# Low parts of the expert weights: GpSimd alone, and the last three experts' behind the block table

## The chip, the core and the metric

The kernel runs on one core of a Trainium2 chip. The metric is the device time of one execution in microseconds. Five engines take part: TensorE (PE), VectorE (DVE), ScalarE (ACT), GpSimd (POOL) and SyncE (SP, which here only issues DMAs). Each runs its own queue in order and waits on semaphores.

## The reference

Sixteen images of 96 x 96 are cut into 36 patches each, embedded (width 192) and joined by a class token: 16 x 37 = 592 tokens. One attention block follows (12 heads, causal mask, rotary positions), then a mixture of experts:

```
gates = softmax(x @ Wg + bg);  topk_g, topk_i = top_k(gates, 2)      # 8 experts
h = gelu(x @ W1[e] + b1[e])            # 192 -> 768
y = h @ W2[e] + b2[e]                  # 768 -> 192
out = x + sum over the two chosen experts of gate * y
```

## The kernel before

**Tokens.** The 592 tokens are worked on in TILES = 6 tiles of up to 111 tokens. Embedding, projections and rotary come first, then a software pipeline over the tiles i = 0 to 6, in which each engine's order is written out by hand: scores, softmax, values and output projection of tile i or i - 1, and the second norm and the gating of tile i - 3. The last tiles' gating follows it as a straight chain: `second_stats`, `norm_apply`, `gates_t`, `logits`, `choose`, `ranks`, `rows`.

**Dispatch.** For each tile DVE (`rows`, L1159) finds the row of each chosen (token, expert) pair, and GpSimd scatters the normed tokens to DRAM with two indirect DMAs (`dispatch`, L398, L405), which count up `scattered`. After the last tile DVE computes the block table (L1222 to L1242): how many blocks of 128 rows each expert has, and for each of up to NB = 17 blocks its expert (`T_EXP`) and first row (`T_ROW`). `table_ready` releases the rest. With the inputs used 14 blocks are live.

**Weights.** An expert's weights are 32-bit numbers and are used as a high and a low part: ACT rounds the raw weights to `F32R` (`round_w1`, `round_w2`; semaphores `w1_hi`, `w2_hi`), and the low part is the raw number less the high one. GpSimd makes the low parts of `w2` of all experts (`split_w2`, L380, 1152 columns) and those of `w1` of experts 0 to 4 (`split_w1`, L386 and L388, 768 columns each); both count up `lo_pool`. DVE makes those of `w1` of experts 5, 6 and 7 (its own `split_w1`, L1024 and L1026, `lo_dve`), after the table and ahead of the first block. EARLY = 6 experts are loaded and rounded during the attention; the raw weights of experts 6 and 7 lie where the attention's buffers were and are loaded by SP once `early_free` is set.

**GpSimd's order** (L408 to L449): in loop step i `root` and `dispatch` of tile i - 3 and i - 4 and the splits of expert i - 1; then `root(4)`, the bias rows of experts 6 and 7 (L395, L396, two DMAs that it issues), `split_w2(5)`, `root(5)`, `dispatch(3)` to `dispatch(5)`, `split_w2(6)`, `split_w2(7)`, and then for each block the indirect DMA that adds the block's output into `out` (L446). `root` computes 1/sqrt of the variance, for which DVE waits in `norm_apply` (L1012 to L1015).

**SP after the table:** the stores of `h` (L353), the waits for `scattered` (L356), the loads of the table's values (L305, L360), and then the load of each block's rows into `xin` (L364).

**The blocks.** For block b: TensorE transposes `xin` (`block_t`, L695, L696); ACT rounds it (L935 to L937); DVE makes the low part (`tokens_low`, L1253, L1254, which read PSUM, and set `xlo_ready`); TensorE computes `layer1` (ten matmuls of 384 columns, L708), ACT the gelu (L947), TensorE transposes (`hidden_t`, L718) and computes `layer2` (L732, L734), ACT and DVE make the output (L964, L1281). In DVE's queue `block_gates(b)` stands ahead of `tokens_low(b)`: a copy of the token numbers (L1261), and two small operations whose inputs are all in SBUF (L1262, L1265), for the gates. TensorE loads the block's expert into a register (`expert_of`, L738) a block ahead. While it waits for the table it runs nothing; then come 18 warm-up matmuls (L743), `block_t(0)`, and waits for all low parts of all experts, `lo_dve` for 3 and `lo_pool` for 13.

Of the kernel before, what the change touches and what calls it, by code (L numbers as in the profile page):

```python
# [23 lines left out]
ALU = mybir.AluOpType  # L24
# [11 lines left out]
DA, DB = 128, D - 128  # L36
# [4 lines left out]
E = 8  # L41
F = 768
# [8 lines left out]
NB = (2 * N - E) // BLK + E  # L51
# [4 lines left out]
A_HI, A_LO, B_HI, B_LO, W2_HL = 0, F, 2 * F, 3 * F, 4 * F  # L56
WCOLS = 4 * F + FC * 2 * D
EARLY = 6
# [5 lines left out]
FH = F // 2  # L64
LAG = 3

T_EXP, T_ROW, T_LIVE, T_COLS = 0, NB, 2 * NB, 2 * NB + 1


class Region:  # L70
# [15 lines left out]
def vit_block(nc, patches, w_tok, tok_rows, tok_sel, w_qkv_a, w_qkv_b, rope_cos, rope_sin, mask,  # L86
# [4 lines left out]
    with ctx:  # L91
        def sem(name):
            return ctx.enter_context(nc.semaphore(name))
# [61 lines left out]
        table = keep("table", [128, NB])  # L155
        tablei = keep("tablei", [128, T_COLS], I32)
# [3 lines left out]
        we = Region(nc, w_at, top)("we", [128, E, WCOLS], F32R)  # L160

        raw = [Region(nc, w_at + e * WCOLS * 4, top)(f"raw{e}", [128, WCOLS], F32) for e in range(E)]
# [11 lines left out]
        tmp_nb = scratch("tmp_nb", [128, 2, NB])  # L174
# [96 lines left out]
        table_ready = sem("table_ready")  # L271
        padded = sem("padded")
        w1_hi = sem("w1_hi")
# [2 lines left out]
        b1_raw = sem("b1_raw")  # L276
        b1_lo = sem("b1_lo")
        b1_rows = sem("b1_rows")
        lo_dve = sem("lo_dve")
        lo_pool = sem("lo_pool")  # L280
        early_free = sem("early_free")
        xin_ld = [sem(f"xin_ld{b}") for b in range(2)]
# [19 lines left out]
        def blocks_in_use(engine):  # L302

            engine.wait_ge(table_ready, 1)
            live = engine.value_load(tablei[0:1, T_LIVE:T_LIVE + 1], min_val=MINB, max_val=NB)  # L305
            return lambda b: engine.If(live > b) if b >= MINB else nullcontext()
# [59 lines left out]
        @block.gpsimd  # L366
        def _(pool):
            def root(t, rnd):

                n = ROWS[t]  # L370
                pool.wait_ge(veps_ready, rnd * TILES + t + 1)
                nc.gpsimd.tensor_tensor(rstd[0:n, t:t + 1], veps[0:n, t:t + 1], nhalf[0:n, :], ALU.pow)\  # L372
                    .then_inc(rstd_ready, 1)

            def split_w2(e):

                pool.wait_ge(w2_hi, e + 1)
                hl = we[:, e, W2_HL:WCOLS].rearrange("p (f c) -> p f c", c=2 * D)
                whole = raw[e][:, W2_HL:WCOLS].rearrange("p (f c) -> p f c", c=2 * D)
                nc.gpsimd.tensor_tensor(hl[:, :, D:2 * D], whole[:, :, D:2 * D], hl[:, :, 0:D], ALU.subtract)\  # L380
                    .then_inc(lo_pool, 1)

            def split_w1(e):

                pool.wait_ge(w1_hi, e + 1)
                nc.gpsimd.tensor_tensor(we[:, e, A_LO:A_LO + F], raw[e][:, A_LO:A_LO + F], we[:, e, A_HI:A_HI + F],  # L386
                                        ALU.subtract)
                nc.gpsimd.tensor_tensor(we[0:DB, e, B_LO:B_LO + F], raw[e][0:DB, B_LO:B_LO + F],  # L388
                                        we[0:DB, e, B_HI:B_HI + F], ALU.subtract).then_inc(lo_pool, 1)

            def bias_rows(e0, e1):
                if e1 > EARLY:
                    pool.wait_ge(early_free, 1)

                pool.dma_start(we[DB:DB + 1, e0:e1, B_LO:B_LO + F], b1[e0:e1, :]).then_inc(b1_rows, 16)  # L395
                pool.dma_start(we[DB + 1:DB + 2, e0:e1, B_LO:B_LO + F], b1lo_sb[e0:e1, :]).then_inc(b1_rows, 16)  # L396

            def dispatch(t):  # L398

                n = ROWS[t]  # L400
                pool.wait_ge(row_ready, t + 1)
                if t == 0:
                    pool.wait_ge(padded, 16)
                for j in range(2):
                    pool.indirect_dma_start(xs, bass.IndirectOffsetOnAxis(ap=rowu[0:n, t, j:j + 1], axis=0),  # L405
                                            pay[0:n, t % 3, :], None).then_inc(scattered[t % 3], 16)

            pool.wait_ge(fixed, 1)  # L408
            nc.gpsimd.memset(vp[:, :, :, HD:HD + 1], 1.0).then_inc(ones_ready, 1)
            for t in range(TILES):  # L410
                root(t, 0)
            for t in range(TILES):
                n = ROWS[t]
                pool.wait_ge(rope_ready, t + 1)
                nc.gpsimd.tensor_tensor(qk[0:n, t, :], ropec[0:n, t % 2, :], ropes[0:n, t % 2, :], ALU.add)\
                    .then_inc(qk_ready, 1)
                pool.wait_ge(v2_ready, t + 1)
                nc.gpsimd.tensor_tensor(vp[0:n, t, :, PC:VC],
                                        vr[0:n, t % 2, :].rearrange("p (h d) -> p h d", d=HD),
                                        vp[0:n, t, :, HD + 1:PC], ALU.subtract).then_inc(v3_ready, 1)  # L420
            pool.wait_ge(b1_lo, 1)
            bias_rows(0, EARLY)
            for i in range(TILES + 1):
                if i >= LAG:
                    root(i - LAG, 1)
                if i >= LAG + 1:
                    dispatch(i - LAG - 1)
                if 1 <= i < EARLY:
                    split_w1(i - 1)
                    split_w2(i - 1)  # L430
            root(TILES - 2, 1)
            bias_rows(EARLY, E)
            split_w2(EARLY - 1)
            root(TILES - 1, 1)
            dispatch(TILES - 3)
            dispatch(TILES - 2)
            dispatch(TILES - 1)
            for e in range(EARLY, E):
                split_w2(e)
            pool.wait_ge(out_first, 16 * (TILES + 1))  # L440
            used = blocks_in_use(pool)
            for b in range(NB):
                with used(b):
                    pool.wait_ge(y_ready, b + 1)
                    pool.wait_ge(gate_ready, b + 1)
                    pool.indirect_dma_start(out, bass.IndirectOffsetOnAxis(ap=tokblk[:, b:b + 1], axis=0),  # L446
                                            y[:, b % 2, :], None, compute_op=ALU.add).then_inc(added, 16)

                    pool.wait_ge(added, 16 * (b + 1))  # L449

        @block.tensor
        def _(pe):
# [245 lines left out]
            def layer1(b, expert):  # L698

                pe.wait_ge(xlo_ready, b + 1)  # L700
                for hf in range(2):
                    if b >= 1:
                        pe.wait_ge(gelu_done, 2 * b - 1 + hf)
                    parts = ((xahi, A_HI), (xalo, A_HI), (xahi, A_LO), (xb1, B_HI), (xb2, B_LO))
                    for i, (x, c) in enumerate(parts):
                        rows = x.shape[0]
                        w = we[0:rows, bass.ds(expert, 1), c + hf * FH:c + hf * FH + FH].rearrange("p e c -> p (e c)")
                        last = mm(bank[1 + hf][:, 0:FH], x[:, :], w, start=(i == 0), stop=(i == 4))  # L708
                    last.then_inc(l1_done, 1)
# [33 lines left out]
                mm(bank[3][:, 0:FH], we[:, 0, A_HI:A_HI + 128], we[:, 0, A_HI:A_HI + FH], start=True, stop=True)  # L743
            pe.wait_ge(early_free, 1)
            block_t(0)
            pe.wait_ge(lo_dve, E - EARLY + 1)
            pe.wait_ge(lo_pool, E + EARLY - 1)
            pe.wait_ge(b1_rows, 64)
            expert = expert_of(0)
            layer1(0, expert)  # L750
# [234 lines left out]
        def _(dve):  # L985
            v = nc.vector
            steps = [0]

            def step(ins):
                steps[0] += 1  # L990
                ins.then_inc(dve_step, 1)
                dve.wait_ge(dve_step, steps[0])
# [25 lines left out]
            v.memset(nhalf[:, :], -0.5).then_inc(fixed, 1)  # L1018
            v.memset(hn2tb[DB:DB + 1, :, :], 1.0).then_inc(fixed, 1)

            def split_w1(e):

                dve.wait_ge(w1_hi, e + 1)
                v.tensor_tensor(we[:, e, A_LO:A_LO + F], raw[e][:, A_LO:A_LO + F], we[:, e, A_HI:A_HI + F],  # L1024
                                ALU.subtract)
                v.tensor_tensor(we[0:DB, e, B_LO:B_LO + F], raw[e][0:DB, B_LO:B_LO + F],  # L1026
                                we[0:DB, e, B_HI:B_HI + F], ALU.subtract).then_inc(lo_dve, 1)

            for t in range(TILES + 1):
                if t < TILES:  # L1030
                    dve.wait_ge(h_copied, t + 1)
# [148 lines left out]
            for i in range(TILES + 1):  # L1180
# [29 lines left out]
                if i >= LAG:  # L1210
# [24 lines left out]
            step(v.tensor_reduce(tmp_nb[:, :, :], passed[:, :, :, :], AX.X, ALU.add))  # L1235
            step(v.scalar_tensor_tensor(out=tmp_nb[:, 1, :], in0=blockids_sb[:, :], scalar=float(BLK),
                                        in1=tmp_nb[:, 1, :], op0=ALU.mult, op1=ALU.add))
            v.tensor_scalar(table[:, :], tmp_nb[:, 0, :], float(E - 1), None, ALU.min)
            v.tensor_copy(tablei[:, T_LIVE:T_LIVE + 1], ends[:, E - 1:E])
            v.tensor_scalar(tablei[:, T_EXP:T_EXP + NB], tmp_nb[:, 0, :], float(E - 1), None, ALU.min)  # L1240
            v.tensor_scalar(tablei[:, T_ROW:T_ROW + NB], tmp_nb[:, 1, :], float(SPARE), None, ALU.min)\
                .then_inc(table_ready, 1)  # L1242

            for t in range(TILES - 3, TILES):
                add_bias2(t)

            for e in range(EARLY - 1, E):
                split_w1(e)

            def tokens_low(b):  # L1250

# [130 lines left out]
```

## Time and profile before

| | before |
|---|---|
| time, median of 3 runs | 245.99 us (243.65 to 252.13) |
| the profiled execution | 244.32 us |
| its span | 242.5 us |
| PE / PEld / DVE / ACT / POOL busy | 75% / 58% / 63% / 43% / 40% |
| granted TensorE clock, mean | 0.802 |

The profile's span runs from the first to the last instruction; PEld is TensorE's weight load, which overlaps PE. [...] In the rows below `a<-b` is output and inputs of an instruction by the program's names, `x` a count, and the bracket at the end is the engine's idle time before it and what ended that. All times start at the span's start.

### The profile page before, as it was taken

The numbers are of one execution on the slowest core, as the hardware profiler recorded it, in microseconds if no ns is written. First come the engines' busy times: TensorE is split into PE (matmuls) and PEld (weight loads), VectorE is DVE, ScalarE is ACT, GpSimd is POOL, SyncE is SP. The second block draws the span as 40 slices with busy tenths as digits, with TensorE's granted clock in tenths as the row PEclk, the third lists the DMA queues.
The fourth block names the chain that finished last, engine by engine and source line by source line (L and its number), as shares of the span: only waits on it lengthen the run. The fifth ranks groups of instructions, "written<-read, shape, count | busy, mean of one in ns | idle before, by whom it ended". The sixth has DMA issues, their size and how long they took to land.

```text
span 242.5 us, 3838 instructions
## 1 busy us (share of the span) xinstructions
PE 182.8 (75%) x1065; PEld 140.7 (58%) x1065; DVE 153.4 (63%) x436; ACT 104.4 (43%) x313; POOL 96.1 (40%) x77
## 2 busy tenths in 40 slices
PE   3999999659799499729829343454899999999830
PEld 2887343245666295615815122254799999999720
DVE  0133756859878968797994888996356455564410
ACT  2011333477687366527030022900656566566500
POOL 1012265739404600853925736930023233433241
PEclk9999999977587956955555555559999999999995
DMA  6945999999999400100100795202032342422211
GB/s 164 312 111 138 278 285 279 285 279 251 201 194 210 112 3 1 39 0 4 39 0 13 213 278 143 50 26 76 22 63 38 59 59 42 67 52 20 33 19 16
DMA packets 25656, 27.12 MB, mean 112 GB/s; under 512 B 4880, under 2 KB 21928, under 8 KB 25634
## 3 DMA queue, kind: packets, MB, share of 16 engines
q1 hardware_dynamic: 21378, 24.16, 40.1%
q0 software_dynamic: 4256, 2.69, 7.8%
q8 instruction: 11, 0.18, 0.3%
q14 instruction: 11, 0.09, 0.1%
HBM read 23.73 MB, written 8.64 MB: 133 GB/s over the span
## 4 chain that ended last, share of the span: by engine, by line
PE 50%; DVE 23%; DMA 10%; issue 8%; ACT 3%; SPq 2%; POOL 1%; ACTq 0%; POOLq 0%; DVEq 0%
PE bank L708 8%; DMA out_y<-y,tokblk 7%; PE bank L463 6%; PE bank L534 5%; PE bank L732 4%; PE bank L489 4%; DVE sneg L1091 3%; DVE ao L1118 3%; PE bank L718 3%; DVE tablei L1240 3%; PE bank L495 2%; PE bank L734 2%; PE bank L550 2%; DVE pay L1015 2%; DMA wtok_sb<-in_w_tok 1%
## 5 line engine op out<-in xcount | busy, mean ns | idle before, releaser
L446 POOL DMA_INDIRECT out_y<-y,tokblk x14 | 21.9, 1562 | 55.2 <-DVE y L1281 23.8
L372 POOL TENSOR_TENSOR rstd<-veps,nhalf 111x1 f32<-111x1 f32 (+1 forms) x12 | 7.0, 584 | 58.5 <-DVE veps L999 58.5
L732 PE MATMUL bank<-we,hthi 128*128 x84 | 25.9, 371 | 1.4 <-DVE htlo L1272 1.4
L827 ACT ACTIVATE probs<-bank,sneg 111x111 f32<-111x111 f32 (+1 forms) x72 | 18.2, 347 | 18.2 <-DVE sneg L1091 18.1
L380 POOL TENSOR_TENSOR we<-raw,we 128x1152 fp32r<-128x1152 f32 x8 | 20.9, 2617 | 4.8 <-ACT we L883 4.7
L1091 DVE TENSOR_SCALAR sneg<-smax 111x4 f32<-111x4 f32 (+1 forms) x18 | 21.0, 1166 | 0.6
L708 PE MATMUL bank<-we,xahi 128*128 x56 | 20.2, 361 | 1.4 <-DVE xb L1254 1.4
L405 POOL DMA_INDIRECT dispatched<-pay,rowu x12 | 16.5, 1373 | 11.9 <-DVE rowu L1167 10.1
L734 PE MATMUL bank<-we,htlo 128*128 x84 | 21.1, 251 | 0.0
L463 PE MATMUL bank<-wtok_sb,x_sb 128*111 128x192 f32 (+1 forms) x72 | 17.5, 403 | 4.1 <-DMA wtok_sb<-in_w_tok 4.1
L947 ACT ACTIVATE hid<-bank 128x384 f32<-128x384 f32 x28 | 13.8, 492 | 10.2 <-PE bank L708 10.2
L463 PEld LDWEIGHTS bank<-wtok_sb,x_sb 128*111 128x111 f32 (+1 forms) x72 | 13.9, 208 | 6.7 <-DMA wtok_sb<-in_w_tok 4.7
L550 PE MATMUL bank<-ident_sb,probs 111*111 111x111 f32 (+1 forms) x72 | 13.5, 346 | 5.2 <-ACT probs L827 5.0
L732 PEld LDWEIGHTS bank<-we,hthi 128*128 128x128 f32 x84 | 15.8, 188 | 1.6 <-issue 1.6
L1272 DVE TENSOR_TENSOR htlo<-bank,hthi 128x512 fp32r<-128x512 f32 (+1 forms) x28 | 14.3, 553 | 3.7 <-ACT hthi L955 3.7
L550 PEld LDWEIGHTS bank<-ident_sb,probs 111*111 111x111 f32 (+1 forms) x72 | 11.9, 248 | 8.2 <-ACT probs L827 5.4
L997 DVE BATCH_NORM_STATS2 stats<-h 111x6 f32<-111x192 f32 (+1 forms) x12 | 4.2, 354 | 18.8 <-ACT h L779 18.8
L734 PEld LDWEIGHTS bank<-we,htlo 128*128 128x128 f32 x84 | 16.1, 192 | 0.0
L567 PE MATMUL bank<-vp,pth 111*111 111x33 bf16 (+1 forms) x72 | 12.9, 215 | 3.3 <-issue 3.3
L534 PE MATMUL bank<-kbda,qta 128*111 128x444 f32 (+1 forms) x24 | 15.3, 734 | 0.0
L1281 DVE SCALAR_TENSOR_TENSOR y<-bank,gblk,y 128x192 f32<-128x192 f32 x14 | 5.9, 418 | 14.1 <-ACT y L964 14.1
L708 PE MATMUL bank<-we,xb 128*128 (+1 forms) x56 | 14.5, 341 | 0.0
(162 smaller groups left out, 491.2 us busy)
## 6 DMA issues: line engine op xcount, KB each, us to landing
dispatched<-in_pad_rows SPq DMA_DIRECT2D x1, 5350.5 KB, 37.4
raw<-in_w SPq DMA_DIRECT2D x8, 576.0 KB, 12.8
raw<-in_w_a SPq DMA_DIRECT2D x8, 384.0 KB, 8.9
raw<-in_w_bb SPq DMA_DIRECT2D x8, 384.0 KB, 9.4
xin<-dispatched SPq DMA_DIRECT2D x14, 130.5 KB, 2.1
x_sb<-in_patches SPq DMA_DIRECT2D x5, 333.0 KB, 5.8
raw<-in_w_b SPq DMA_DIRECT2D x8, 192.0 KB, 9.1
wtok_sb<-in_w_tok SPq DMA_DIRECT2D x3, 192.0 KB, 3.5
```

Source lines behind the costliest of these rows:

```text
L380: nc.gpsimd.tensor_tensor(hl[:, :, D:2 * D], whole[:, :, D:2 * D], hl[:, :, 0:D], ALU.subtract)\
L405: pool.indirect_dma_start(xs, bass.IndirectOffsetOnAxis(ap=rowu[0:n, t, j:j + 1], axis=0), pay[0:n, t % 3, :], None).then_inc(scattered[t ...
L446: pool.indirect_dma_start(out, bass.IndirectOffsetOnAxis(ap=tokblk[:, b:b + 1], axis=0), y[:, b % 2, :], None, compute_op=ALU.add).then_in ...
L463: mm(bank[t][0:n, 0:D], x_sb[:, t, k, 0:n], wtok_sb[:, k, :], start=(k == 0), stop=False)
L534: mm(o, q, k, start=True, stop=False)
L550: last = tr(bank[3 + i % 2][0:n, TOK * j:TOK * j + n], probs[0:n, b, HG * g + j, 0:n], ident_sb[0:n, 0:n])
L708: last = mm(bank[1 + hf][:, 0:FH], x[:, :], w, start=(i == 0), stop=(i == 4))
L732: mm(o[:, 0:2 * D], hthi[:, f, :], w, start=(f == 0), stop=False)
L734: last = mm(o[:, 0:D], htlo[:, f, :], w, start=False, stop=(f == FC - 1))
L827: last = fn(probs[0:n, b, hd, 0:n], bank[g][0:n, TOK * j:TOK * j + n], ACT.Exp, bias=sneg[0:n, b, hd:hd + 1], scale=float(HD) ** -0.5)
L1091: v.tensor_scalar(sneg[0:n, b, hs], smax[0:n, b, hs], -float(HD) ** -0.5, None, ALU.mult)\
L1272: v.tensor_tensor(htlo[:, f0:f1, :], bank[3 + q][:, 0:(f1 - f0) * 128].rearrange("p (f s) -> p f s", s=128), hthi[:, f0:f1, :], ALU.subtra ...
```

## The change

GpSimd makes all low parts. Its `split_w2(5)` leaves its place ahead of `root(5)`. Behind the last dispatch it waits for `table_ready` and then runs `split_w1(e)` and `split_w2(e)` for the experts 5, 6 and 7 in turn. DVE's `split_w1` and `lo_dve` go. The table gets a third row, `T_NEED`: for each block 2 * expert + 2, the value of `lo_pool` at which that expert's low parts are complete. `layer1` loads it into a register of TensorE's and waits for it, block by block, and the wait for all experts' goes.

```diff
-T_EXP, T_ROW, T_LIVE, T_COLS = 0, NB, 2 * NB, 2 * NB + 1
+T_EXP, T_ROW, T_NEED, T_LIVE, T_COLS = 0, NB, 2 * NB, 3 * NB, 3 * NB + 1
...
             root(TILES - 2, 1)
             bias_rows(EARLY, E)
-            split_w2(EARLY - 1)
             root(TILES - 1, 1)
             dispatch(TILES - 3)
             dispatch(TILES - 2)
             dispatch(TILES - 1)
-            for e in range(EARLY, E):
+            pool.wait_ge(table_ready, 1)
+            for e in range(EARLY - 1, E):
+                split_w1(e)
                 split_w2(e)
...
             def layer1(b, expert):
 
                 pe.wait_ge(xlo_ready, b + 1)
+                pe.wait_ge(lo_pool, pe.value_load(tablei[0:1, T_NEED + b:T_NEED + b + 1], min_val=2, max_val=2 * E))
...
             block_t(0)
-            pe.wait_ge(lo_dve, E - EARLY + 1)
-            pe.wait_ge(lo_pool, E + EARLY - 1)
             pe.wait_ge(b1_rows, 64)
...
-            def split_w1(e):
-
-                dve.wait_ge(w1_hi, e + 1)
-                v.tensor_tensor(we[:, e, A_LO:A_LO + F], raw[e][:, A_LO:A_LO + F], we[:, e, A_HI:A_HI + F],
-                                ALU.subtract)
-                v.tensor_tensor(we[0:DB, e, B_LO:B_LO + F], raw[e][0:DB, B_LO:B_LO + F],
-                                we[0:DB, e, B_HI:B_HI + F], ALU.subtract).then_inc(lo_dve, 1)
...
-            v.tensor_scalar(table[:, :], tmp_nb[:, 0, :], float(E - 1), None, ALU.min)
+            step(v.tensor_scalar(table[:, :], tmp_nb[:, 0, :], float(E - 1), None, ALU.min))
             v.tensor_copy(tablei[:, T_LIVE:T_LIVE + 1], ends[:, E - 1:E])
             v.tensor_scalar(tablei[:, T_EXP:T_EXP + NB], tmp_nb[:, 0, :], float(E - 1), None, ALU.min)
+            v.tensor_scalar(tablei[:, T_NEED:T_NEED + NB], table[:, :], 2.0, 2.0, ALU.mult, ALU.add)
...
-            for e in range(EARLY - 1, E):
-                split_w1(e)
```

## Rows read from the trace of the kernel before

**Rows 1.** Busy time by stretch: span, length, then PE, PEld, DVE, ACT, POOL, clock, DMA.

```profile
170.00:200.00 30.00, 28.94 (x200) 28.44 (x199) 15.32 (x51) 18.82 (x56) 7.89 (x5) 1.00 0.28 49
```

**Rows 2.** Timeline around the block table: start, us, engine, line, operation, output and inputs.

```profile
153.49 1.34 POOL L405 DMA_INDIRECT dispatched<-pay,rowu  x1 [0.30 <-issue]
153.88 6.21 DVE L1240 TENSOR_SCALAR tablei<-tmp_nb 128x17 int32<-128x17 f32 x1
154.86 5.19 POOL L380 TENSOR_TENSOR we<-raw,we 128x1152 fp32r<-128x1152 f32 x2
```

**Rows 3.** The chain that ended last, from SP's wait to the first blocks: start, us, what.

```profile
161.98 0.03 SPq L356
...
164.84 1.96 DMA xin<-dispatched
...
168.75 2.03 PE bank L708 x10
...
172.94 1.77 PE bank L708 x10
```

**Rows 4.** Timeline, 135 to 146 us.

```profile
135.77 3.44 DVE L1015 TENSOR_SCALAR pay<-h,mv,rstd 111x64 f32<-111x64 f32 x1
...
136.50 2.64 POOL L380 TENSOR_TENSOR we<-raw,we 128x1152 fp32r<-128x1152 f32 x1
...
145.24 1.15 ACT L883 ACTIVATE we<-raw 128x1152 fp32r<-128x1152 f32 x1
```

**Rows 5.** Timelines of DVE and POOL, DVE beside GpSimd's splits.

```profile
58.06 0.82 DVE L1091 TENSOR_SCALAR sneg<-smax 111x4 f32<-111x4 f32 x1
...
101.02 0.36 DVE L1117 TENSOR_TENSOR ao<-bank,ao 111x192 f32<-111x192 f32 x1
101.41 5.40 DVE L1118 TENSOR_TENSOR ao<-ao,rsum 111x192 f32<-111x192 f32 x1
...
100.45 1.82 POOL L386 TENSOR_TENSOR we<-raw,we 128x768 fp32r<-128x768 f32 x1
102.22 1.81 POOL L388 TENSOR_TENSOR we<-raw,we 64x768 fp32r<-64x768 f32 x1
103.97 2.62 POOL L380 TENSOR_TENSOR we<-raw,we 128x1152 fp32r<-128x1152 f32 x1
```

**Rows 6.** Timeline of DVE, its last split and the first block's own work.

```profile
165.22 0.94 DVE L1026 TENSOR_TENSOR we<-raw,we 64x768 fp32r<-64x768 f32 x1
...
166.89 0.21 DVE L1262 SCALAR_TENSOR_TENSOR gsel<-xin,table 128x2 f32<-128x2 f32 x1
167.13 0.16 DVE L1265 TENSOR_TENSOR gblk<-gsel 128x1 f32<-128x1 f32 x1
...
168.31 0.29 DVE L1254 TENSOR_TENSOR xb<-bank,xb 64x128 fp32r<-64x128 f32 x1
```

**Rows 7.** DMA issues, 153 to 162 and 133.5 to 135.9: KB, us to landing.

```profile
dispatched<-pay,rowu POOLq DMA_INDIRECT x2, 4.7
...
raw<-in_w SPq DMA_DIRECT2D x1, 576.0 KB, 6.9
```

**Rows 8.** TensorE's register load (ns, min/median/max), and the timeline before a later `layer1`.

```profile
L738 PEldq TENSOR_LOAD <-tablei x17: 296/302/492, 167.1 to 232.3; - x17
L738 PEldq FUSED_REGOPS  x17: 151/151/160, 167.6 to 232.7; - x17
...
180.41 0.29 DVE L1254 TENSOR_TENSOR xb<-bank,xb 64x128 fp32r<-64x128 f32 x1
...
181.39 0.42 PE L708 MATMUL bank<-we,xahi 128*128 x1
```

**Rows 9.** Busy time by stretch again: an idle one, a long dense one, the warm-up.

```profile
86.00:90.00 4.00, 4.00 (x32) 4.00 (x31) 1.89 (x11) 2.17 (x11) 0.00 (x0) 0.50 0.00 0
...
103.00:104.00 1.00, 0.00 (x0) 0.00 (x0) 1.00 (x1) 0.00 (x0) 1.00 (x2) 0.50 0.00 1
...
160.16:163.60 3.44, 3.38 (x11) 3.38 (x12) 3.44 (x8) 0.00 (x0) 0.00 (x0) 0.50 0.14 41
```

More of the change, by code:

```diff
@@ L278, in vit_block @@
         b1_rows = sem("b1_rows")
-        lo_dve = sem("lo_dve")
         lo_pool = sem("lo_pool")
```

## The prediction

> **What bounds the kernel now.** I read the page first (its busy shares and its chain), then the chain of waits in order of time, then the timeline around each long piece of it. In the last third TensorE is the bound: it computes for 28.94 of 30 us at full clock, block after block [rows 1]. So whatever moves the start of the first block's `layer1` moves the end by as much, and the question is what sets that start, 168.75 [rows 3].
>
> Two stalls of VectorE stand in the chain ahead of it. The first is the block table. L1240, a tiny operation on 17 columns, begins at 153.88 and takes 6.21 us: GpSimd's descriptor work (L405, to 154.83) and then its two `split_w2` (to 160.05) come first, so that it ends at 160.09, and L1241 and with it `table_ready` follow at once [rows 2]. The second lies earlier: L1015 begins at 135.77 and takes 3.44 us, while GpSimd issues the bias loads (to 136.50) and then runs `split_w2(5)` to 139.14 [rows 4]. From the table to the first block the chain goes through SP: it is past the `scattered` waits at 161.98, issues the load of `xin` at 164.84, which lands at 166.80, and `layer1(0)` starts at 168.75 [rows 3]. The waits on the low parts (`lo_dve`, `lo_pool`) don't set it: DVE's last split ends at 166.16, before `xin` lands [rows 3, 6].
>
> What the stalls have in common: while GpSimd runs a split, DVE operations with both inputs in SBUF, or a plain scalar operation SBUF to SBUF, stand still, and those that read PSUM run. L1117 (PSUM) takes 0.36 us beside a split; L1118 (both inputs in SBUF) takes 5.40 us and ends when the third split does [rows 5].
>
> **The change, part by part.** The sum is made on the profiled execution (244.32 us, span 242.5); the median of the three runs shown is 245.99, 0.7% more.
>
> *`split_w2(5)` leaves its place ahead of `root(5)`.* L1015 then waits at most for the bias loads' issue (L395, L396), whose end is the start of the old split, 136.50, and not for 139.14: -2.6 us [rows 4]. The work after it is a chain of DVE, TensorE, ACT and GpSimd that shifts as a whole. One load could hold it: ACT's `round_w2(6)` needs `raw6`, whose last part is issued by 135.9 and lands 6.9 us after its issue, by 142.8 [rows 7]; its turn moves from 145.24 to 142.6 [rows 4]. It just fits, so nothing is charged.
>
> *The last splits wait for the table.* L1240 now waits for L405 alone, so it ends at 154.83 where it ended at 160.09: -5.2; the added `step` and the `T_NEED` operation stand beside L405's end or cost 0.1. Together -2.6 - 5.1 = -7.7: `table_ready` at 152.4. This is the gain.
>
> *The first `xin`.* Behind the stores of `h`, SP's next wait is `scattered`. The last scatter starts at 153.49 - 2.6 = 150.9 and lands 4.7 us later, 155.6 [rows 2, 7]; before, this wait cost nothing, now it does. From there to the landed `xin` are 166.80 - 161.98 = 4.8 us [rows 3]: 160.4.
>
> *GpSimd's stream.* From 152.5 on it runs, back to back, three experts' splits. One expert is 1.77 + 1.75 + 2.61 = 6.13 us by the starts and the last end of the three [rows 5]; three are 18.4 us, to 170.9. All their inputs are ready: before, GpSimd had split expert 7's `w2` by 160.05 [rows 2], and ACT rounds that last. The low parts themselves are not late: with the routing of these inputs, worked out from the reference, the 14 live blocks go to experts 0, 1, 1, 2, 3, 3, 4, 5, 5, 6, 6, 6, 6, 7, so that block 7 is the first that waits for a late split, some 30 us after the first; expert 5 is complete at 158.6.
>
> *Who stands behind the stream.* DVE's six `split_w1` operations (0.94 us each by the last [rows 6]) go; they hid under SP's path, so that is worth nothing. But `xin` lands at 160.4, inside the stream, and the next DVE work is `block_gates(0)`: L1262 and L1265, both with two SBUF inputs, the kind of L1118. They stand ahead of `tokens_low(0)`, which reads PSUM and could run, but it is behind them in DVE's queue, and TensorE waits for it. I take it that they wait until the stream ends, as L1118, L1015 and L1240 did. Then `xlo_ready` comes at 170.9 + 0.24 (L1262 to L1265) + 0.16 + 0.6 (the two of `tokens_low`) = 171.9 [rows 6], and `layer1` 0.14 later as before, 172.0.
>
> *The new register load.* `layer1` now loads `T_NEED` behind its wait for `xlo_ready`. The like load of L738 is 0.30 + 0.15 us and small gaps [rows 8], about 0.6 with the wait. For block 0 it lies bare: `layer1(0)` at 172.7, +3.9 against 168.75. In the later blocks there is slack: `xlo_ready` comes at 180.70, `layer1` could start 0.13 later, and starts at 181.39 because TensorE is still busy [rows 8]; 0.13 + 0.64 against 0.69 leaves 0.1 us a block, 12 times 1.2; block 1 has less cover, 0.3. Together +1.5. Bounds: nothing, and all of it 14 times, 9.0.
>
> *The clock.* After the warm-up and `block_t(0)` TensorE idles from 160.9 to 172.7. In an idle stretch the granted clock stood at half (0.50 from 103 to 104, without a matmul), and the warm-up ran at half for the 3.44 us before it rose, 11 matmuls of the same 384 columns [rows 9], 3.44 / 11 = 0.31 us each. At that pace the ten matmuls of `layer1(0)` take 3.1 us in place of 1.8 [rows 3]: +1.3 at least. Dense work also ran at half for longer, as in 86 to 90, where TensorE was busy throughout [rows 9]; if it lasted 9 us, half of it would be lost, 4.5. I take 2.0, near the lower end, because large matmuls like the warm-up's follow.
>
> Sum: 244.3 + 3.9 + 1.5 + 2.0 = **251.7 us**, 3.0% above the same execution.
>
> **A rule beside the rows.** DVE waited out a boundary between two GpSimd instructions 12 times of 13, counted over seven waits (L1118, L1015 and L1240 are three of them); the one where it got in is the L1091 at 58.06, which ended at the boundary at 58.88 after 0.82 us [rows 2, 5].
>
> [...]
>
> **The rivals.**
> *DVE gets in between two splits.* By the spacing above GpSimd's instructions start at 160.4, 162.2, 164.8; L1262 runs at 162.2, L1265 at 164.8, `layer1(0)` at 164.8 + 0.16 + 0.6 + 0.14 + 0.6 = 166.3, -2.4. With +1.5 and +2.0: 245.4. For it: the L1091 at 58.06. Against: the other twelve.
> [...]
> *The register load isn't covered at all*, with the stall: 244.3 + 3.9 + 2.0 + 9.0 = 259.2. Against it: the slack in [rows 8].
>
> **How the numbers follow.** Stall to the end of the stream 0.65 (its own range 248.5 to 256: clock 1.3 to 4.5, loads 0 to 3, the first wait 1 us either way), between two splits 0.12, no stall 0.17, bare loads 0.06. The time predicted is the first's. The range goes from 241 (half of "no stall" is below) to 257.5 (most of "bare loads" is above), 0.15 left out. Two per cent is about what a measurement tells here: 249.2 against 244.3. Slower by more: nearly nine tenths of the first and the last, 0.64. Within 2%: the rest of the first, the between, over half of "no stall", 0.28. Faster: the rest, 0.08.
>
> **What would show it.** L1015 under 0.8 us; L1240 ends with L405; `table_ready` about 152.4; nine GpSimd splits back to back for 18.4 us; L1262 (or the copy ahead of it) of some 10 us that ends with the last split; `layer1(0)` at 172.7 at half clock; gaps of 0.1 us ahead of each later `layer1`. An L1262 of 0.2 us, or one that ends at an inner boundary, would make the prediction wrong, and so would a `layer1` of the later blocks held by its register load.

## The result, and the profile after

| | before | after |
|---|---|---|
| time, median | 244.82 us (4 runs, 243.4 to 252.13) | 249.56 us (4 runs, 247.84 to 249.94) |
| the profiled execution | 244.32 us | 249.94 us |
| its span | 242.5 us | 248.1 us |
| granted TensorE clock, mean, as a share of full speed | 0.802 | 0.782 |

The ratio to before is 1.0148, 95% interval 1.0082 to 1.0213: slower by more than the noise. The medians of the table alone would give 1.019 and the profiled pair gives 1.023, so the loss is 1.5% to 2.3%, half to three quarters of the 3.0% that was forecast. By its ratio it lies just within the 2% that the prediction gave 0.28, and not in the "slower by over 2%" that it gave 0.64. Some executions come out over 1.5% above the fastest of their kernel; the ratios in this document leave these out, the medians don't.

The steps ahead of the stream came as foretold. The timeline of the kernel after, VectorE first (L1014 is the L1015 of before, L1231 and L1233 its L1240 and L1241, L1251 and L1254 its L1262 and L1265, L1243 its L1254):

```profile
136.10 0.31 DVE L1014 TENSOR_SCALAR pay<-h,mv,rstd 111x64 f32<-111x64 f32 x1
...
151.22 0.17 DVE L1231 TENSOR_SCALAR tablei<-tmp_nb 128x17 int32<-128x17 f32 x1
...
151.37 0.66 DVE L1233 TENSOR_SCALAR tablei<-tmp_nb 128x17 int32<-128x17 f32 x1
...
159.69 0.15 DVE L1250 COPY tokblk<-xin 128x1 uint32<-128x1 uint32 x1 [7.38 <-DMA xin<-dispatched]
159.76 6.43 DVE L1251 SCALAR_TENSOR_TENSOR gsel<-xin,table 128x2 f32<-128x2 f32 x1
166.23 1.72 DVE L1254 TENSOR_TENSOR gblk<-gsel 128x1 f32<-128x1 f32 x1
...
168.17 0.29 DVE L1243 TENSOR_TENSOR xb<-bank,xb 64x128 fp32r<-64x128 f32 x1
...
168.56 1.97 DVE L1251 SCALAR_TENSOR_TENSOR gsel<-xin,table 128x2 f32<-128x2 f32 x1
```

L1014 takes 0.31 us where L1015 took 3.44 [rows 4], and the table is complete at 152.03 instead of after 160.09 [rows 2]. The load of `xin` lands at 159.69, seven microseconds earlier [rows 3]. Then L1251, which took 0.21 us before [rows 6], takes 6.43, L1254 takes 1.72 instead of 0.16, and everything that the table had won is gone. GpSimd's timeline in the same kernel shows whom they wait for:

```profile
152.12 1.83 POOL L385 TENSOR_TENSOR we<-raw,we 128x768 fp32r<-128x768 f32 x1
...
160.06 1.79 POOL L387 TENSOR_TENSOR we<-raw,we 64x768 fp32r<-64x768 f32 x1
161.82 2.60 POOL L379 TENSOR_TENSOR we<-raw,we 128x1152 fp32r<-128x1152 f32 x1
164.38 1.80 POOL L385 TENSOR_TENSOR we<-raw,we 128x768 fp32r<-128x768 f32 x1
166.14 1.80 POOL L387 TENSOR_TENSOR we<-raw,we 64x768 fp32r<-64x768 f32 x1
167.90 2.62 POOL L379 TENSOR_TENSOR we<-raw,we 128x1152 fp32r<-128x1152 f32 x1
```

The nine splits run from 152.12 to 170.52, 18.4 us without a gap. L1251 ends at 166.19, where the eighth split begins, having passed the starts of three others (160.06, 161.82, 164.38); L1254 ends at 167.95, where the ninth begins.

The chain of the kernel after from the first block on (start, us, what; L709 is `layer1`, L719 the transposes of `hidden_t`):

```profile
169.27 3.56 PE bank L709 x10
...
174.32 1.54 PE bank L719 x6
175.86 2.61 PE bank L709 x10
...
181.04 2.00 PE bank L709 x10
```

`layer1(0)` starts at 169.27, 0.5 later than before [rows 3], and runs at half the clock (0.50 for 1.00): 3.56 us where ten matmuls took 2.03. The stretches say so too (span, length, busy times of PE, PEld, DVE, ACT and POOL, the granted clock, and two numbers on the DMAs, as in [rows 1]):

```profile
161.00:169.00 8.00, 0.00 (x0) 0.00 (x0) 7.92 (x6) 0.00 (x0) 8.00 (x5) 0.50 0.00 0
169.20:173.00 3.80, 3.73 (x12) 3.50 (x12) 1.49 (x2) 0.49 (x1) 1.32 (x1) 0.50 0.11 33
173.00:177.50 4.50, 3.44 (x14) 3.18 (x13) 1.95 (x7) 1.84 (x6) 0.00 (x0) 0.50 0.12 30
177.50:180.90 3.40, 3.40 (x25) 3.27 (x24) 0.61 (x4) 1.92 (x7) 0.00 (x0) 0.98 0.17 44
```

TensorE stands still from 161 to 169 and then works at 0.50 until 177.5. Even at full clock the blocks are further apart than before. In the timeline, at two of the later ones:

```profile
185.62 0.44 PE L709 MATMUL bank<-we,xahi 128*128 x1
...
194.81 0.19 PEld L709 LDWEIGHTS bank<-we,xahi 128*128 128x128 f32 x1 [0.26 <-issue]
...
231.42 0.44 PE L709 MATMUL bank<-we,xahi 128*128 x1
```

From block 3 to block 13 that is 45.80 us, 4.58 a block. In the kernel before, block 3 starts at 181.39 [rows 8] and block 13 here:

```profile
224.93 0.43 PE L708 MATMUL bank<-we,xahi 128*128 x1
```

That is 43.54 us, 4.35 a block. In front of each `layer1` TensorE's weight load now stands idle 0.19 to 0.26 us, for "issue".

**Where the 5.6 us of the profiled pair went.** The table and L1015 gave 8.1, and `xin` 7.1 of them. `layer1(0)` starts 0.5 later. From it to block 3 it took 12.64 us before (168.75 to 181.39) and takes 16.35, 3.7 more: clock and three register loads. Ten more blocks add 2.3. The tail behind the first matmul of block 13 is 0.9 shorter (17.6 to 16.7). 0.5 + 3.7 + 2.3 - 0.9 = 5.6. So 0.5 us of the loss stand ahead of `layer1(0)` and 5.1 behind it.

### The profile page after: what moved, and what is told of

The parts are those of the page before. It is cut to its first block, busy times and chain, and to the rows that moved or that the text cites. A ratio compares the mean times of both kernels' runs of the same rounds, so it can differ in the third digit from the quotient of the medians.

```text
span 248.1 us, 3881 instructions
## 1 busy us (share of the span) xinstructions
PE 189.6 (76%) x1065; PEld 144.5 (58%) x1065; DVE 148.6 (60%) x431; ACT 104.6 (42%) x313; POOL 106.6 (43%) x83
## 4 chain that ended last, share of the span: by engine, by line
PE 56%; DVE 19%; issue 8%; DMA 7%; ACT 3%; POOL 2%; SPq 1%; ACTq 0%; POOLq 0%; DVEq 0%
PE bank L709 11%; PE bank L463 6%; PE bank L733 6%; PE bank L534 5%; PE bank L489 4%; PE bank L719 4%; DVE sneg L1082 3%; DMA out_y<-y,tokblk 3%; DVE ao L1109 3%; PE bank L735 3%; DVE gsel L1251 3%; PE bank L495 2%; PE bank L550 2%; DMA dispatched<-pay,rowu 2%; POOL dispatched L404 2%
## 5 line engine op out<-in xcount | busy, mean ns | idle before, releaser
L709 PE MATMUL bank<-we,xahi 128*128 x56 | 21.7, 387 | 9.1 <-DVE xb L1243 9.1
L709 PEld LDWEIGHTS bank<-we,xahi 128*128 128x128 f32 x56 | 11.5, 206 | 11.8 <-issue 11.8
L709 PE MATMUL bank<-we,xb 128*128 (+1 forms) x56 | 15.4, 358 | 0.0
L567 PE MATMUL bank<-vp,pth 111*111 111x33 bf16 (+1 forms) x72 | 12.8, 215 | 3.3 <-issue 3.3
```

## The experiments

Four questions: is the stall of the gates' operations what eats the gain; what the register load and the clock cost by themselves; what each half of the change does alone; and when VectorE gets in. All ratios are to the kernel before, on the same chip.

**Gates by one column at a time.** The kernel after, and in `block_gates`:

```diff
-                step(v.scalar_tensor_tensor(out=gsel[:, b % 2, :], in0=x[:, C_IDX:C_IDX + 2],
-                                            scalar=table[:, b:b + 1], in1=x[:, C_GATE:C_GATE + 2],
-                                            op0=ALU.is_equal, op1=ALU.mult))
-                v.tensor_tensor(gblk[:, b:b + 1], gsel[:, b % 2, 0:1], gsel[:, b % 2, 1:2], ALU.add)\
+                for j in range(2):
+                    last = v.tensor_scalar(gsel[:, b % 2, j:j + 1], x[:, C_IDX + j:C_IDX + j + 1], table[:, b:b + 1],
+                                           x[:, C_GATE + j:C_GATE + j + 1], ALU.is_equal, ALU.mult)
+                step(last)
+                v.tensor_scalar(gblk[:, b:b + 1], gsel[:, b % 2, 0:1], gsel[:, b % 2, 1:2], None, ALU.add)\
```

> The kernel after, but block_gates computes the gates with four VectorE operations on one column each (tensor_scalar with one SBUF tensor input and its scalars as pointers) in place of L1251 (two columns, two tensor inputs) and L1254 (two tensor inputs). Theory 1 (the stall is VectorE's need for a second input from SBUF, or the wide form of a scalar operation, beside GpSimd's splits; the one-column copy L1250 wasn't held in the kernel after): block_gates(0) takes under 1 us at 159.8, xlo_ready comes 1.8 us behind the landed xin as in the kernel before, at 161.5, layer1(0) at 162.3 in place of 169.27, 7.0 less. The clock term stays about as it is. Time 7.0 below the kernel after's: ratio to before about 0.985. Rival 1 (any VectorE operation that takes more than one operand from SBUF, scalar pointers too, is held): the column operations end at a boundary between two splits like L1251, layer1(0) stays at 167 to 171, ratio 1.01 to 1.02.

Measured: 242.19 us, ratio 0.9869 (0.9825 to 0.9913), 1.3% faster than before. Its timeline, VectorE and GpSimd:

```profile
159.52 1.79 POOL L387 TENSOR_TENSOR we<-raw,we 64x768 fp32r<-64x768 f32 x1
159.52 0.45 DVE L1252 TENSOR_SCALAR gsel<-xin,table 128x1 f32<-128x1 f32 x2
...
160.00 0.21 DVE L1255 TENSOR_SCALAR gblk<-gsel 128x1 f32<-128x1 f32 x1
...
160.94 0.29 DVE L1243 TENSOR_TENSOR xb<-bank,xb 64x128 fp32r<-64x128 f32 x1
...
162.04 0.68 PE L709 MATMUL bank<-we,xahi 128*128 x1 [2.07 <-POOL we L387]
```

Here the same arithmetic takes 0.45 and 0.21 us while a split runs, and `layer1(0)` starts at 162.04, 7.2 earlier than in the kernel after; the time is lower by the same amount. So the stall is the reason that the change lost, and not the amount of work on GpSimd, which is unchanged. L1254 had one column too, with two tensors as inputs, and was held (1.72 us); L1255, one column with its second number as a scalar pointer, isn't (0.21 us). (The bracket names L387, GpSimd's split, since its semaphore came last by the profile; `lo_pool` for block 0 was long there, and VectorE's L1243 is what released it.)

**The load a block ahead.** The kernel after, with `T_NEED` loaded beside `T_EXP` in `expert_of`, and in `layer1`:

```diff
                 pe.wait_ge(xlo_ready, b + 1)
-                pe.wait_ge(lo_pool, pe.value_load(tablei[0:1, T_NEED + b:T_NEED + b + 1], min_val=2, max_val=2 * E))
+                pe.wait_ge(lo_pool, need)
```

> The kernel after, but TensorE loads T_NEED beside the block's expert, a block ahead, and layer1 only waits. Theory 1 (the load behind xlo_ready costs 0.23 us in each block, 4.59 in place of 4.355 from layer1 to layer1, and 0.65 in front of layer1(0)): the distance goes back to 4.36 to 4.40, layer1(0) starts 0.65 earlier behind xlo_ready; together 0.65 + 12 x 0.2 = 3.0 less, ratio to before 1.00. Rival 1 (the wait on a register, or GpSimd's work in the blocks, makes the distance): 4.59 stays, ratio 1.015.

Measured: 246.64 us, ratio 1.0057 (1.0018 to 1.0095). It is 0.9 points below the kernel after, 2.2 us, where 3.0 were expected. The profiled execution took 250.62 us, 4 above the median, so only distances are read from it. `layer1(0)` follows `tokens_low` within 0.15 us, for 0.81 in the kernel after, and the distance is back at 4.35:

```profile
170.92 0.31 DVE xb L1244
...
171.36 3.56 PE bank L709 x10
...
183.25 1.78 PE bank L709 x10
...
187.60 1.77 PE bank L709 x10
```

So the load behind `xlo_ready` made the gap, and the wait on a register by itself costs nothing that shows (in the kernel before it was 0.14 us and 4.35). That the gain is less than 3.0 isn't shown: the intervals of the two ratios leave about 1.8 us either way (an estimate from their widths), and the two medians lie 2.9 apart. A shortfall would fit the 0.9 by which the tail of the kernel after was shorter, since the output's DMAs on GpSimd, 4.4 to 4.6 us apart at the end of both kernels, cover part of the slower blocks; no run separates it.

**`split_w2(5)` moved, alone.** The kernel before, with this split behind the dispatches and no wait for the table.

> The kernel before, but split_w2(5) runs behind the dispatches, ahead of split_w2(6), and nothing waits for the table. Theory 1 (VectorE waits out GpSimd's splits wherever they lie): L1015 takes 0.3 in place of 3.44, all behind it is 2.6 earlier, and L1240 waits through three splits in place of two, 2.6 longer: table_ready stays at 160, ratio 1.00. If VectorE gets in at a boundary between two splits: table_ready at 152.3 + 2.6 or 5.2, ratio 0.98 to 0.99. Rival 1 (the stall of L1015 was no part of the chain's length): the table is 2.6 later, ratio 1.01.

Measured: 245.29 us, ratio 0.9935 (0.9860 to 1.0011): no difference that can be told from none. The timeline shows why, give and take:

```profile
135.70 0.31 DVE L1014 TENSOR_SCALAR pay<-h,mv,rstd 111x64 f32<-111x64 f32 x1
...
150.69 8.77 DVE L1239 TENSOR_SCALAR tablei<-tmp_nb 128x17 int32<-128x17 f32 x1
```

Of the 3.1 us that L1014 no longer waits, 2.6 are paid by L1239, which now waits through three splits, 8.77 us where it was 6.21 [rows 2]. The stall was moved here, not removed: a VectorE operation on the path stood beside the stream either way.

**The wait for the table, alone.** The kernel before, with `pool.wait_ge(table_ready, 1)` ahead of `split_w2(6)` and `split_w2(7)`; all other splits where they were.

> The kernel before, but GpSimd waits for the table before split_w2(6) and split_w2(7). VectorE's split_w1 stay, and so does the wait for all low parts. Theory 1: L1240 ends with the last dispatch at 154.9, table_ready 155.1 in place of 160.2. VectorE's six splits (two SBUF inputs) are held by GpSimd's two until 160.4 at the latest and then take 5.2 us, to 165.6; xin lands at 163.0 (the scatters' landing, 158.2, plus 4.8); block_gates(0) at 165.7, layer1(0) at 166.9 in place of 168.75: 1.8 less, ratio 0.993. If VectorE gets in at the boundary between the two: 2 to 3 less, 0.99. Rival 1 (the moment of table_ready doesn't reach the first block): ratio 1.00.

Measured: 245.13 us, ratio 0.9975 (0.9924 to 1.0025); 0.993 was expected and is inside the interval, and so is no change. L1242, the last table operation, takes 0.17 us, and then VectorE's own first split, which has two SBUF inputs, stands in for the gates:

```profile
156.72 1.34 POOL L405 DMA_INDIRECT dispatched<-pay,rowu  x1 [0.30 <-issue]
...
157.11 0.17 DVE L1241 TENSOR_SCALAR tablei<-tmp_nb 128x17 int32<-128x17 f32 x1
157.18 0.17 DVE L1242 TENSOR_SCALAR tablei<-tmp_nb 128x17 int32<-128x17 f32 x1
...
158.05 6.11 DVE L1025 TENSOR_TENSOR we<-raw,we 128x768 fp32r<-128x768 f32 x1
```

L1025 is a third VectorE instruction that waits for the stream's end (it ends at 164.16, GpSimd's two splits at 163.33, and the five others of VectorE's splits, beside no split of GpSimd's, take 0.94 each).

```profile
169.54 3.56 PE bank L709 x10
```

The gain did reach the first block, and the clock took most of it. Counted from the start of the last scatter, `layer1(0)` begins after 12.8 us (156.72 to 169.54) where it was 15.3 (153.49 to 168.75), 2.4 earlier. But TensorE had paused for longer on either side of `block_t(0)` (3.19 and 2.35 us, 1.70 and 1.41 before), `layer1(0)` runs at half clock (0.50; 3.56 us for 2.03), and the second block's `layer1` follows 5.84 us behind it where it was 4.19 [rows 3]: 1.65 of the 2.4 are gone. The 0.8 that are left are 0.3%, which fits the ratio.

**Both edits.** Columns and load ahead together.

> The kernel after with both edits: gates by operations on one column (as in e1_columns) and T_NEED loaded a block ahead (as in e2_load_ahead). Theory 1 (the stall and the load are two separate costs): the effects add, 0.987 less 0.009: ratio to before 0.978, layer1 to layer1 4.35. Rival 1 (they cover each other, since TensorE's spare time would wait for something else): ratio 0.987, as e1_columns.

Measured: 240.30 us, ratio 0.9803 (0.9753 to 0.9854). The effects add. Its `layer1` of the first and of the third block:

```profile
160.89 3.56 PE bank L709 x10
...
172.68 1.78 PE bank L709 x10
```

**A longer warm-up in the kernel after** (76 matmuls for 18).

> The kernel after with 76 warm-up matmuls in place of 18, so that TensorE works until about 166.5 and is at full clock when layer1(0) starts. Theory 1 (the clock costs what layer1(0), the transposes and layer1(1) took more: 1.5 + 0.7 + 0.6 = 2.8 us): layer1(0) takes 2.0 in place of 3.56, ratio to before 1.0148 - 0.0115 = 1.003. Rival 1 (the longer warm-up delays block_t(0), or the clock costs less because VectorE's stall on block_gates(1), to 170.7, is waited for anyway): ratio 1.01 to 1.015.

Measured: 248.53 us, ratio 1.0138 (1.0058 to 1.0217). Theory 1 fell and the rival's 1.01 to 1.015 came, and the stretches show where:

```profile
161.00:167.00 6.00, 6.00 (x37) 6.00 (x36) 5.96 (x2) 0.00 (x0) 6.00 (x4) 1.00 0.01 3
167.60:169.50 1.90, 0.00 (x0) 0.00 (x0) 1.41 (x5) 0.55 (x3) 1.90 (x2) 1.00 0.22 69
169.50:172.70 3.20, 3.11 (x11) 3.02 (x12) 0.97 (x2) 0.49 (x1) 0.79 (x1) 0.60 0.00 1
```

TensorE is at full clock until 169.5, but after a pause of 2 us it falls to half during `layer1(0)` (0.76 in its first microsecond, 0.50 from 170.6 to 172.7), which takes 3.14 us, and is back at full for that of the next block (1.00, 2.02 us). This run avoids the long half-speed stretch only in part, and delays `block_t(0)` by the rest of the warm-up. It doesn't size the clock term.

**A longer warm-up with both edits** (38 matmuls).

> As e5_both, with 38 warm-up matmuls in place of 18, until about the time that xin lands. Theory 1: the clock stays up into layer1(0), 2.0 to 2.8 us less than e5_both: ratio to before 0.968. Rival 1 (the pause between warm-up and layer1(0) still lets the clock fall): as e5_both, 0.978.

Measured: 237.86 us, ratio 0.9706 (0.9653 to 0.9759), 2.9% faster than before. Its chain and one stretch:

```profile
151.06 9.09 PE bank L745 x38
...
161.78 2.02 PE bank L709 x10
...
165.96 1.75 PE bank L709 x10
...
170.28 1.78 PE bank L709 x10
```

```profile
161.70:170.30 8.60, 7.46 (x49) 7.16 (x50) 3.70 (x15) 4.42 (x14) 8.02 (x4) 1.00 0.15 44
```

`layer1(0)` starts 0.9 later than in the run of both edits (161.78 against 160.89), because `block_t(0)` waits for the warm-up, and yet the time is 2.4 us lower. So the half-speed stretch costs about 2.4 + 0.9 = 3.3 us there. The chains agree: from the first to the third block's `layer1` it is 11.79 us in the run of both edits and 8.50 here.

**A shorter one** (30 matmuls), to have the 0.9 back.

> As e7_both_warm, with 30 warm-up matmuls in place of 38. In e7_both_warm they ended at 160.15, 1.5 us behind the landed xin (158.66), and block_t(0) waited for them. Theory 1: 8 fewer take 1.4 us less, block_t(0) follows xin at once, layer1(0) starts up to 1.4 earlier, and the clock still stays up: ratio to before 0.965 to 0.968. Rival 1 (the pause of 2 us in front of layer1(0) is then long enough for the clock to fall): ratio 0.975 to 0.98.

Measured: 237.68 us, ratio 0.9710 (0.9642 to 0.9779), the same as with 38; the interval takes in both forecasts, so the trace has to decide. `layer1(0)` starts at 159.92, 1.9 earlier (0.7 of it because `xin` lands earlier in this execution), and the gain is eaten by the clock, which fell to 0.5 behind it (0.54 over the stretch here, 0.50 from 165 to 168, where the second block's `layer1` takes 3.04 us):

```profile
161.00:165.00 4.00, 2.94 (x14) 2.44 (x13) 0.59 (x2) 1.46 (x5) 4.00 (x3) 0.54 0.14 33
```

**A GpSimd operation that reads nothing between the splits.** The kernel after, with a memset of one column ahead of each late split.

> The kernel after with a GpSimd memset of one column (an instruction that reads nothing) ahead of each of the late splits. In the kernel after, L1251 waited through the ends of three splits and got in at the fourth. Theory 1 (VectorE misses its turn only because the next split claims the read side at once): with the memset between, L1251 gets in at the first end, 160 to 162, L1254 at the next, layer1(0) at 163 to 166 in place of 169.27, ratio to before about 1.00. Rival 1 (the turn goes by GpSimd's queue whatever stands in it): L1251 ends at 166 or later, ratio 1.015.

Measured: 248.84 us, ratio 1.0146 (1.0050 to 1.0242), over two executions. Theory 1 fell; the rival's ratio came, but not its L1251 that ends at 166 or later (here it is L1258). Two lines of its timeline:

```profile
158.43 4.39 DVE L1258 SCALAR_TENSOR_TENSOR gsel<-xin,table 128x2 f32<-128x2 f32 x1
162.86 3.54 DVE L1261 TENSOR_TENSOR gblk<-gsel 128x1 f32<-128x1 f32 x1
```

Each of the two passed one boundary with a memset in it and got in at the second (162.8 and 166.4). The memset doesn't reliably let VectorE in.

**`tokens_low` ahead of `block_gates`**, for the first two blocks, in the kernel after; the gates' operations unchanged.

> The kernel after with tokens_low(0) and tokens_low(1) ahead of block_gates(0) and block_gates(1) in VectorE's queue; the gates' operations are as in the kernel after. Theory 1 (tokens_low was late only because it stood behind the held gates): layer1(0) starts about 162.3 in place of 169.27, as in e1_columns; but then hidden_low(0), needed at about 168.5, stands behind the two held gates, to 170.5 at most, so that part of the gain is lost: ratio to before 0.99 to 1.00. Rival 1 (tokens_low itself is held by GpSimd's splits): layer1(0) at 167 or later, ratio 1.015.

Measured: 244.38 us, ratio 1.0027 (0.9976 to 1.0078). `layer1(0)` starts at 160.90 in the profile, so `tokens_low` was late only by its place in the queue, and its operations, one input from PSUM and one from SBUF, aren't held (0.29 us each, beside splits that run from 158.04 to 162.42). Part of the gain is lost behind the gates, in VectorE's timeline and in the chain:

```profile
166.19 0.15 DVE L1250 COPY tokblk<-xin 128x1 uint32<-128x1 uint32 x1
166.26 2.35 DVE L1251 SCALAR_TENSOR_TENSOR gsel<-xin,table 128x2 f32<-128x2 f32 x1
```

```profile
169.02 2.01 DMA xin<-dispatched
```

The third block's `xin` is loaded only at 169, because SP waits for the first block's gate, and `layer1` of that block for it. The gate is late by the edit itself, which puts `block_gates(0)` behind `tokens_low(1)` (to 166.15), and then by the ninth split (to 168.6). Counted from the start of the last scatter (148.68 here, 150.70 in the kernel after), `layer1(0)` is 6.4 us earlier than there and the third block's `layer1` (173.87 against 181.04) 5.2. Those 5.2 us would be a ratio of 0.994 (an estimate); what takes the other 2 us, about as much as the two intervals leave open, isn't shown.

## Why the prediction was right and wrong, step by step

- **`split_w2(5)`**: right. L1014 took 0.31 us. It wasn't even held by the bias loads' issue, which the prediction had allowed: -3.1 for the operation, not -2.6. It began 0.3 later, and the last scatter starts 2.8 earlier (150.70 for 153.49).
- **The table**: right. 152.03 for 152.4. The reading of its stall wasn't: L1240 began 0.39 us into L405 and took 6.21, which was put down to the descriptor work first and the splits then. In the run with the wait alone the same operation began 0.39 us into L405 too, with no split free to follow, and took 0.17. So it was the splits behind L405 that held it, from before they ran. The two halves need each other: the move alone hands its gain to the table's stall, the wait alone hands it to VectorE's own splits and to the clock.
- **`xin`**: 159.69 for 160.4, right. The scatters' landing did set it: the chain of the kernel after goes through it (4.67 us from 150.70).
- **The stream**: 18.4 us, exact. No block waited for its low parts.
- **Who is held**: right in kind and in place, L1251 and L1254, and the experiment with columns proves it. The one-column copy ahead of them wasn't held (0.15 us).
- **How long they are held**: this is the step that was mis-sized. The prediction let them wait to the end of the stream, 170.9, and so set `layer1(0)` at 172.7; they got in at boundaries between splits, and `layer1(0)` came at 169.27. The term was +0.5 and not +3.9, an error of 3.4 us. The rival "between two splits" (166.3) erred the other way. "No stall" (0.17, and half of it set the range's lower end of 241) didn't come either, since L1251 took 6.43 us; no run shows the kernel after without the stall at 241, and the one with the gates by columns took 242.19. Counted over these two operations of block 0, VectorE got in at 2 of 5 starts of a following split in the kernel after and at 2 of 4 in the one with the memsets, against 1 of 13 in the trace before. The runs with the load ahead and with 76 warm-up matmuls held the same two operations and add 2 of 4 each, at the same places as the kernel after: the starts of the eighth split (168.90 and 165.90) and of the ninth (170.66 and 167.68). The twelve misses before were taken as a rule, and they weren't one; but three kernels that agree on the place don't look like chance either. What decides it, no run shows.
- **The register load**: +0.67 for block 0 (0.81 us from `xlo_ready` to `layer1` for 0.14), as foretold (0.64). In the later blocks it was 0.23 and not 0.1: 13 x 0.23 = 3.0 where the prediction had 1.5. The tail gave 0.9 back, which it hadn't foreseen. The run with the load ahead gives back 2.2, give or take 1.8, of 0.67 + 3.0 - 0.9 = 2.8. (The rival with bare loads, 259.2, counts block 0's load twice, in the 3.9 and in the 9.0; it should be 258.6.)
- **The clock**: 2.0 was predicted; 3.7 - 3 x 0.23 = 3.0 by the ledger above, 3.3 by the runs with both edits. Half speed (0.50) lasted 8.2 us from the start of `layer1(0)`, not about 4. It was inside the range given (1.3 to 4.5), and the reason for taking the lower end (that large matmuls follow) was wrong.
- **The sum**: 251.7 against 249.94 for the profiled execution. The errors were -3.4 (stall), +1.5 (loads), +1.0 (clock) and -0.9 (tail), together -1.8, and they cancelled in part. The prediction had 3.9 us ahead of `layer1(0)` and 3.5 behind it; the trace has 0.5 and 5.1. The direction was right for the right reason, since without the stall the same kernel is 1.3% faster than before; the nearness of the number was in part luck.

## What to carry to other kernels

Work that is moved to GpSimd to free VectorE isn't beside VectorE for every operation. What ran beside the splits here took one tensor from SBUF at most: `tokens_low`, with its other input in PSUM (0.29 us), the one-column copy (0.15), and single columns with scalar pointers (0.45 for two, and 0.21). What was held took two tensors from SBUF (L1251 6.43 us, L1254 1.72, L1118 5.40 [rows 5]) or was a plain scalar operation from SBUF to SBUF on several columns (4, 17 and 64: 0.82, 6.21 and 3.44 us [rows 5, 2, 4]). Look for the few of these kinds, however small, and for what is queued behind them. Here two operations of 0.2 us held TensorE for 7 us, and rewriting them on single columns turned a loss of 1.5% into a gain of 1.3%, with the loads and the warm-up put right 2.9%. A register load belongs ahead of the last wait, not behind it (behind it, it cost 0.67 us in front of `layer1(0)` and 0.23 a block). And the gap that opened in front of the dense stretch cost twice, once for itself and once for the clock (about 3 us).

## What the runs showed of the hardware that was not expected

- A VectorE operation that waits for GpSimd's splits sometimes gets in between two of them and sometimes doesn't. L1251 passed three starts and got in at the fourth (6.43 us), L1254 at its first (1.72 us), L1091 before at its first (0.82 us [rows 5]). A GpSimd memset in the gap didn't make it regular. What decides it stays open. By these traces it is mostly GpSimd that goes on (at 12 of 13 starts before, 3 of 5 in the kernel after). An earlier start didn't help L1240 either: it began 0.98 us ahead of the first of the two splits and waited for both [rows 2].
- In three of the kernels the two got in at the same starts, those of the eighth and the ninth split (after, load ahead, 76 warm-up matmuls); with the memsets it was the seventh and the ninth.
- A VectorE operation can be held by a split that hasn't begun. With splits next in GpSimd's queue L1240 took 6.21 us from 0.39 us into L405, and 0.17 from the same point where GpSimd had to wait for the table. In the same way L1015, beside the bias loads' issue, took 3.44 us with `split_w2(5)` behind them, before and in the run with the wait alone, and 0.31 without it, in the kernel after and in the run with the move alone. The descriptor work by itself held only what began later in it: in the kernel after L1231, 0.52 us into it, took 0.17, and L1233, 0.67 into it, took 0.66.
- `tensor_scalar` on one column with two scalar pointers isn't held (0.45 us for two), while a `tensor_scalar` with constants on 17 columns is (L1239, 8.77 us, through three splits). These two differ in their scalars too; no run varies the columns alone.
- With both edits, the pauses in front of `layer1(0)` were 0.55 and 1.41 us (on either side of `block_t(0)`) behind 30 warm-up matmuls, and the clock fell to half within `layer1(0)` (1.00 from 160 to 161, 0.50 from 161.4 to 162.4); behind 38 there was only the second, also 1.41 us, and it stayed at full (1.00 from 161.7 to 170.3). Behind 76, with 2.07 us, it fell within `layer1(0)` (0.50 from 170.6). In the kernel before they were 1.70 and 1.41 behind 18, and it stayed at full (1.00 from 165 to 180.9). The last pause is the same in three of these and the clock isn't, so more than it decides; what, these runs don't say.
